# Products of probabilities and values in groups of four heads, exponentials in a ring of eight tiles (attentions 0 and 2 of a four-layer decoder)

## What is computed

```
x = x + tanh(g_xattn[0]) * L0_xattn(layernorm(x), ctx, ctx, mask, ...)   # attention 0: softmax over keys, masked
x = x + tanh(g_ffn[0])   * L0_ffn(layernorm(x), ...)                     # experts choose tokens
x = x + tanh(g_xattn[1]) * L1_xattn(layernorm(x), ctx, ctx, ...)         # attention 1: softmax over heads
x = x + tanh(g_ffn[1])   * L1_ffn(layernorm(x), ...)                     # int8 product
x = x + tanh(g_xattn[2]) * L2_xattn(layernorm(x), ctx, pad, ...)         # attention 2: softmax over keys, padded
x = x + tanh(g_ffn[2])   * L2_ffn(layernorm(x), ...)                     # ternary layers
x = x + tanh(g_xattn[3]) * L3_xattn(layernorm(x), ctx, ...)              # attention 3: softmax over queries
x = x + tanh(g_ffn[3])   * L3_ffn(layernorm(x), ...)                     # two of eight experts

# attentions 0 and 2, 16 heads of width 16:
scores  = einsum('bhqd,bhkd->bhqk', Q, K) / 4      (masked places: -inf)
weights = softmax(scores, axis=-1)
out     = einsum('bhqk,bhkd->bhqd', weights, V)    then @ Wo.T
```

## Time and profile before

| what | us |
|---|---|
| runs, median of 3 | 2509.2 |
| runs, lowest and highest | 2507.66, 3518.86 |
| span of the profiled execution (its own time is given as this span) | 2506.0 |
| TensorE products busy | 2005.9 (80%) |
| TensorE weight loads busy | 1280.2 (51%) |
| VectorE busy | 1279.5 (51%) |
| ScalarE busy | 810.5 (32%) |

### The profile page before, as it was taken

How to read it: one execution, slowest core, us unless ns; L and a number is a source line. 1 busy time by engine, 2 the same in 40 slices (tenths; PEclk the granted TensorE clock), 3 DMA queues, 4 the chain that set the end, 5 groups by cost and what they waited for, 6 DMA issues and landing times.

```text
span 2506.0 us, 33028 instructions
## 1 busy us (share of the span) xinstructions
PE 2005.9 (80%) x11527; PEld 1280.2 (51%) x11528; DVE 1279.5 (51%) x2283; ACT 810.5 (32%) x1752; POOL 242.8 (10%) x234
## 2 busy tenths in 40 slices
PE   5999983594767755478998999999996676399998
PEld 3556543473534533334444444444444444389997
DVE  5334325516998997844442545453536666522221
ACT  3343331122433422334443521111115765122221
POOL 1010100341000000020110000000001000023333
PEclk9999995796878877579999999999998987599999
DMA  4342305126224210144431400000005541642222
GB/s 109 46 57 32 52 8 215 26 36 130 33 30 54 30 26 5 40 52 59 60 40 13 186 1 1 1 1 1 1 1 93 80 63 26 239 131 38 35 36 30
DMA packets 91386, 132.86 MB, mean 53 GB/s; under 512 B 13428, under 2 KB 80508, under 8 KB 88060
## 3 DMA queue, kind: packets, MB, share of 16 engines
q1 hardware_dynamic: 75900, 103.84, 19.7%
q0 software_dynamic: 15360, 27.28, 6.9%
HBM read 64.09 MB, written 16.26 MB: 32 GB/s over the span
## 4 chain that ended last, share of the span: by engine, by line
PE 59%; DVE 19%; DMA 8%; issue 6%; ACT 4%; SPq 4%; DVEq 0%; POOL 0%; POOLq 0%; ACTq 0%
PE ps L1137 13%; PE ps L808 10%; PE ps L1215 6%; PE ps L1226 5%; DMA Qpack<-QP 3%; PE ps L852 3%; PE ps L771 3%; PE ps L799 2%; DVE hpart L1821 2%; DVE hsum L1826 2%; DMA Kpack<-pad_rows 2%; SPq L446 2%; PE ps L1047 2%; PE ps L1037 2%; PE ps L1111 2%
## 5 line engine op out<-in xcount | busy, mean ns | idle before, releaser
L808 PE MATMUL ps<-pT,V 128*32 128x256 f32 x1536 | 298.5, 408 | 40.3 <-DVE V L1759 40.3
L1740 DVE TENSOR_REDUCE mx<-ps 128x2 f32<-128x512 f32 x256 | 165.6, 686 | 169.4 <-PE ps L774 92.5
L1337 ACT ACTIVATE pT<-ps 128x512 f32<-128x512 f32 x256 | 150.5, 597 | 243.2 <-PE ps L802 140.7
L799 PE MATMUL ps<-Qpack,Kpack 99*128 99x256 bf16 (+1 forms) x768 | 168.2, 289 | 40.5 <-ACT pT L1342 16.6
L808 PEld LDWEIGHTS ps<-pT,V 128*32 128x32 f32 x1536 | 104.7, 112 | 163.2 <-issue 63.3
L1215 PEld LDWEIGHTS ps<-xgT,XNT 128*128 128x128 f32 x1280 | 151.4, 194 | 2.0
L1215 PE MATMUL ps<-xgT,XNT 128*128 128x128 f32 x1280 | 151.5, 277 | 0.0
L1226 PE MATMUL ps<-w,mid 128*128 x640 | 144.6, 379 | 0.0
L771 PE MATMUL ps<-Kpack,Qpack 97*128 97x256 bf16 x512 | 107.9, 287 | 40.8 <-DMA Kpack<-pad_rows 22.7
L1342 ACT ACTIVATE pT<-ps,nmax 128x256 f32<-128x256 f32 x256 | 118.0, 496 | 56.5 <-DVE nmax L1750 55.7
L799 PEld LDWEIGHTS ps<-Qpack,Kpack 99*128 99x128 bf16 (+1 forms) x768 | 70.3, 102 | 123.1 <-ACT pT L1337 42.9
(11 more groups left out here) (312 smaller groups left out, 3733.0 us busy)
## 6 DMA issues: line engine op xcount, KB each, us to landing
Qpack<-QP SPq DMA_DIRECT2D x192, 128.0 KB, 6.9
w<-in_w SPq DMA_DIRECT2D x19, 1024.0 KB, 6.8
Kpack<-KP POOLq DMA_DIRECT2D x96, 128.0 KB, 5.6
Kpack<-KP SPq DMA_DIRECT2D x96, 128.0 KB, 4.2
ctxT<-in_ctxT SPq DMA_DIRECT2D x32, 256.0 KB, 5.9
h<-in_h SPq DMA_DIRECT2D x2, 4096.0 KB, 22.2
wd<-in_wd SPq DMA_DIRECT2D x4, 1536.0 KB, 14.9
xn_rows<-xn SPq DMA_DIRECT2D x16, 256.0 KB, 2.8
```

Source lines behind the costliest of these rows:

```text
L799: mm = pe.matmul(A[h % ring][:, t], Kpack[par][0:rows, h, t * P:(t + 1) * P], Qpack[par][0:rows, h], start=True, stop=L != 0)
L808: mm = pe.matmul(O[c // 2][r0:r0 + VW, c % 2], V[par][:, t, h], weights[:, t], start=t == 0, stop=t == ST - 1)
L1337: act.activation(pT[h % 4][:], A[h % 2][:], ACT.Exp).then_inc(s["exp_done"], 1)
L1740: dve.tensor_reduce(mx[:, :, h], A[2 + h % 2][:], AX.X, ALU.max).then_inc(s["smax_done"], 1)
```

## The change

In attentions 0 and 2 `values` takes a group c of four heads instead of one head. TensorE issues group 0 after the scores of head 7, group 1 after head 11, group 2 after head 15, and group 3 at the end, after `max_turn`; before, head h-2 stood behind the scores of each head h and the last two at the end. The group waits for the exponentials of its four heads. The exponentials go to eight tiles in turn instead of four, and the exponential of head h waits for `values` of head h-8 instead of h-4. Attention 3 calls the same function with the same order and waits as before.

```diff
--- before.py
+++ after.py
@@ -809,19 +809,20 @@
                                        start=t == 0, stop=t == ST - 1)
                     mm.then_inc(done, 1)
 
-                def values(b, par, h):
+                def values(b, par, c):
+
                     if keys:
-                        if h == 0 and L == 0:
+                        if c == 0 and L == 0:
                             pe.wait_ge(s["v_copied"], 8 * i + b + 1)
-                        elif h == 0:
+                        elif c == 0:
                             pe.wait_ge(s["v_ready"], v_before + b + 1)
-                        pe.wait_ge(s["exp_done"], 16 * (8 * s_order[L] + b) + h + 1)
+                        pe.wait_ge(s["exp_done"], 16 * (8 * s_order[L] + b) + GROUP * (c + 1))
                     else:
-                        if h == 0:
+                        if c == 0:
                             wait(pe, s["on_ready"], 8 * i + b)
-                        if h % GROUP == 0:
-                            pe.wait_ge(s["vs_ready"], 4 * b + h // GROUP + 1)
-                    weighted(b, par, h, pT[h % (4 if keys else 8)], s["av_done"])
+                        pe.wait_ge(s["vs_ready"], 4 * b + c + 1)
+                    for h in range(GROUP * c, GROUP * (c + 1)):
+                        weighted(b, par, h, pT[h % 8], s["av_done"])
 
                 def output_turn(b):
 
@@ -923,8 +924,8 @@
                         output_turn(b - 1)
                     for h in range(H):
                         scores(b, par, v, h)
-                        if h >= 2:
-                            values(b, par, h - 2)
+                        if h % GROUP == GROUP - 1 and h > GROUP:
+                            values(b, par, h // GROUP - 1)
                         if h == 3 and before:
                             output_back(b - 1)
                         if h == 7 and before:
@@ -937,8 +938,7 @@
                             proj_q(b + 2)
                     if exists(b + 1):
                         max_turn(b + 1)
-                    for h in range(H - 2, H):
-                        values(b, par, h)
+                    values(b, par, CH - 1)
 
                 def slot1(b, par, v):
 
@@ -981,10 +981,8 @@
                             if c == 3 and exists(b + 2):
                                 query_product(b + 2, k // 2, k % 2)
                         if c:
-                            for h in range(GROUP * (c - 1), GROUP * c):
-                                values(b, par, h)
-                    for h in range(H - GROUP, H):
-                        values(b, par, h)
+                            values(b, par, c - 1)
+                    values(b, par, CH - 1)
 
                 slots(pe, slot_keys if keys else slot1 if L == 1 else slot3)
                 if keys:
@@ -1333,8 +1331,8 @@
                     q = 16 * (8 * s_order[L] + b) + h
                     if keys:
                         act.wait_ge(s["st_ps"], q + 1)
-                        wait(act, s["av_done"], q - 3)
-                        act.activation(pT[h % 4][:], A[h % 2][:], ACT.Exp).then_inc(s["exp_done"], 1)
+                        wait(act, s["av_done"], q - 7)
+                        act.activation(pT[h % 8][:], A[h % 2][:], ACT.Exp).then_inc(s["exp_done"], 1)
                     else:
                         act.wait_ge(s["nmax_ready"], 16 * b + h + 1)
                         wait(act, s["av_done"], q - 7)
```

## The result

The kernel after takes 2463.1 us (median of 4 runs, 2460.78 to 2466.56) where the one before takes 2508.4: a ratio of 0.983, with a 95% interval of 0.9814 to 0.9846. The 2508.4 is the median of four runs with one of 3518.86 us among them that is far from the rest; without it the median is 2507.7. So the change gains some 45 us by the medians, 1.7% by the ratio: a gain, clear of the noise, but short of the 2% (50 us) that the forecast stood just past. The profiled execution took 2460.78, its span is 2459.0 (2506.0 before), 47.0 us less.

A forecast was written before the change was run, and what follows sets the result against it. Transfers Qpack<-QP were taken to bound each slot's opening, TensorE the rest. Savings of 22.4 + 9.6 us (attention 0) and 13.6 + 7.7 (attention 2), together 53.3, took 2509.2 to 2456 us; range 2430 to 2490.

The forecast's parts named there:

- What bounds it: In a batch's slot, transfers Qpack<-QP end the opening stretch (part A, 14.6 us); the rest (part B, 25.8 us) is all TensorE.
- A group costs 1.03 us for 3.92: Values in attentions 0 and 2: four heads issued together take 1.03 us instead of 4 x 0.98 = 3.92.
- The estimate from the Trainium skill: Values groups: 2.38 times for three column tiles, scaled to four, makes a group 1.24 us and the sum 13 us smaller.
- Part A, arrival at 10 and 9.4 us, waits of 4.5 and 5.4: Slot's start to L771's transfer wait, attentions 0 and 2: TensorE arrives sooner, waits 4.5 and 5.4 us; no gain.
- Part B of attention 0: From the end of L771's transfer wait to the slot's end: 25.8 us falls to 20.5, saving 5.3; bounds 3.5 to 6.3.
- The stalls that were walked out: Attention 0, part B, heads 7 to 15: TensorE stalls of 0.3, 0.2 and about 0.4 us at VectorE's row maxima.
- Part B of attention 2, 17.6 + 2.1 = 19.7: After L771's transfer wait: 20.5 us falls to 17.6, set by VectorE, saving 2.9; plus 2.1 for the clock's fall.
- The clock falls in all fourteen, 2.1 us each: Behind L771's wait in attentions 0 and 2, first seven slots each: TensorE's clock falls, costing 2.1 us; bounds 0 and 3.3.
- Rival 1: First seven slots of attentions 0 and 2: the clock is not lost, 21 us more gain, 2435 us; chance 0.12.
- Rival 2: Attention 2's part B: clock stays low or falls again, about 4.6 us in each of seven slots, 32 us, 2488; chance 0.17.
- Rivals 3 to 6: Transfers end sooner, 2366 (0.04); clock stays low, 2639 (0.03); heads don't overlap, 2505 (0.04); slots stall longer, 2477 (0.05).
- Together 53.3 us: Sum over attentions 0 and 2: 22.4 plus 9.6, and 13.6 plus 7.7 us saved, with nothing elsewhere changed.

The follow-up runs named there:

- 5: Kernel after, with the output projection of b-1 and query projection of b+2 moved ahead of L771 and the residual ahead of the first two maxima: 2396.4 us, 0.9558.
- 7: Kernel after, the six transfers Qpack<-QP sending one head of each pair for batches 2 to 7 of attentions 0 and 2: 2409.2 us, 0.9613.
- experiment 4: Kernel after, with 34 products into a free PSUM bank ahead of L771 in each of the fourteen loading slots: 2425.7 us, 0.967.
- warm: Kernel after, with the 34 products that change no result put between the scores of head 6 and L771: 2425.7 us, 0.967.
- Pad: Kernel after, with eight never-waiting waits (four compiled instructions) on TensorE ahead of the ternary feed-forward stage: 2456.5 us, 0.9795.

## Why the prediction was right

- **What bounds it.** Right: the transfers end part A (14.6 us before, 14.5 after, 14.4 in 5), and fewer bytes shorten it (11.0 in 7). In three slots of experiment 4 TensorE, at the low clock, came later than they.
- **A group costs 1.03 us for 3.92.** Right. The slot's last group starts at 164.05 and the next slot at 165.07, 1.02 us later. The estimate from the Trainium skill ("TensorE: Matmul & The Clock Gate", Part 3; 1.24 us, 13 us less gain) didn't come: the attention terms sum to 53.0.
- **Part A, arrival at 10 and 9.4 us, waits of 4.5 and 5.4.** Right. All waits at L771 in the seven slots of attention 0 together, from the view of waits after (us in total, times, longest):

```profile
PE ps L771 <- DMA Qpack<-QP: 31.5, 7, 5.1
```

4.5 each. In attention 2 the seven are 4.87 to 6.10 us.
- **Part B of attention 0.** 20.5 us without the clock's loss; shown by warm, 20.4. The stalls that were walked out, about 0.9 us, are of the right size: between the starts of its products there, the row-maximum products come 0.89 us late in sum.
- **Part B of attention 2, 17.6 + 2.1 = 19.7.** The seven slots have 17.3 (the first), 21.7, 19.6, 19.4, 19.5, 18.9 and 18.7 us. The 17.6 is shown by the 17.5 of warm, though the walk behind it is off by half a microsecond: 5.45 and sixteen operations of 0.60 are 15.05, not 15.5. VectorE is what is late there. The view of waits for these seven slots:

```profile
PE ps L771 <- DMA Kpack<-pad_rows: 26.7, 5, 6.1
PE ps L771 <- DVE mx L1738: 15.0, 50, 1.6
```

15.0 us of waiting for row maxima in fifty places, where the same view has one of 0.9 us for attention 0. The first row is five of the seven waits for transfers, 5.3 us each.
- **The clock falls in all fourteen, 2.1 us each.** Right in number. In size 2.1 us is the mean that warm gives for attention 0; single slots differ (part B of attention 0 was 21.8 to 23.3 us beside 20.4 without a fall: 1.4 to 2.9). For attention 2 it is an inference from single slots of the same work: three with one fall have 19.4 to 19.6 us, the one of warm without 17.5. The prediction counted five falls there before the change, behind waits of 1.7 to 3 us. There are five, but one of them lies in a slot whose wait was 0.45 us, ahead of that wait; that it cost 1.6 us is not shown. The Trainium skill's rule that spoke against the change ("TensorE: Matmul & The Clock Gate", section "HAM oscillation — how this bites in real kernels": bursts with waits for a DMA between them start each time at the low clock) agrees with the trace: each of the fourteen bursts behind a wait starts at 0.50. Rival 1 fell with that.
- **Rival 2**, a second fall in attention 2's part B, was given 32 us and 0.17. It came in one of the seven slots (the one of 21.7 us) and in the last one. The window of it:

```profile
1117.50:1120.50 3.00, 3.00 (x23) 1.26 (x22) 1.47 (x4) 0.60 (x1) 0.00 (x0) 0.50 0.00 0
```

It cost some 2 us in that slot. In the last slot of attention 2, scores to the end of values took 15.5 us where 14.8 was predicted, at the low clock for one stretch:

```profile
1302.00:1305.00 3.00, 3.00 (x20) 1.28 (x21) 0.00 (x0) 1.08 (x2) 0.00 (x0) 0.50 0.00 0
```
- **Rivals 3 to 6.** The waits are there (3 fell), the clock comes back within part B (4), groups overlap (5), slots are not longer than worked out (6).
- **What was missing.** The step "Together 53.3 us" took everything outside the two attentions as unchanged. It isn't: 6 us came back in the ternary stage through the place of its loop in TensorE's program. Pad restores it and lands at 2456.5. That this is the forecast to half a microsecond is luck: the forecast started from 2509.2, and the kernel before has 2507.5 in pad's rounds. Nothing in the diff's meaning tells it; the rows of before did show that two waits of over 4 us there have no releaser, and the sum should have carried a bound for them. So the direction and the range held, the chance of "faster" by over 2% hung on 50 of 53 us, and these six decided against it.

## What to carry to other kernels

Work taken from TensorE ahead of a wait that a transfer sets buys nothing there and costs clock behind it; look at once for work of the next part that can stand in the hole (here two projections, 111 us together with the grouping where the two alone sum to 66). Read where a stage's end is set before and after the change, and treat a gain as open until the idle time that it makes has been given something to do. And when instructions are added or removed, look at long waits without a releaser at the head of loop passes everywhere in the program, and compare the number of instruction packets on the two pages: both moved here, for nothing that the change means.

## What the runs showed of the hardware that was not expected

- The first product of a loop pass waited 2.7 to 7.9 us with no releaser in the profile, and the length depends on the number of instructions ahead: four fewer brought two waits from 8.6 to 15.6 us in total, four without work brought them back to 8.6. Where the waits are long the run has 88 instruction packets of 16,384 bytes for 86, and the product starts 2.3 to 2.8 us after one of them has landed; where they are short it starts before that packet lands.
- The clock is lost not only in full waits. In attention 2's part B the granted clock was 0.52 (window of experiment 4) with TensorE waiting for VectorE between its products; at that clock they take twice their time, so the row still shows it busy 2.74 of 3.00 us. Filling the wait gained only 0.3 us a slot in attention 2, where the clock also fell ahead of the filling and behind it, and 2.1 in attention 0.
- Transfers within the chip's SBUF of 128 KB each, twelve of them beside a load of 256 KB, filled 14.4 us at 129 GB/s with a DMA share of 0.95. Taking 384 KB (393,216 bytes) off, with as many packets, took 3.4 us off, 116 GB/s, near the same rate.
- Adding work can gain time: 34 products that compute nothing, some 3.7 us of TensorE time (34 x 0.11) at full clock in each of fourteen slots, made the kernel 37 us faster, of which the slots themselves show 17. In three slots they met the low clock, took 6.0 to 6.7 us and made part A longer.
